# Scores 0 and 1 of an attention tile moved ahead of the transposes of the samples on TensorE

## What is computed

```python
# layer 0: group norm, then a deformable 3x3 convolution: for each pixel and each of 9 taps
offset = conv(x, offset_w) + offset_b         # where to sample
x_off  = g_lt*gather(..) + g_rb*gather(..) + g_lb*gather(..) + g_rt*gather(..)
x = x + conv2d(x_off, conv_w, K, 0)
# layer 1: tokens t (8, 3136, 128)
q, k, v = ln(t) @ Wq.T, ln(t) @ Wk.T, ln(t) @ Wv.T
scores  = where(causal, q @ k.T * C ** -0.5, -inf)
t = t + softmax(scores) @ v
t = t + ffn(ln(t))        # 64 experts, each pools its top 8 tokens of an image
```

## Time and profile before

| what | value |
|---|---|
| median of 3 runs | 4461.97 us (4454.56 to 4466.91) |
| the profiled execution | 4458.19 us |
| its span, first to last instruction | 4456.4 us |
| mean granted TensorE clock | 0.855 of full speed |
| PE busy | 3340.2 us |
| DVE busy | 2008.4 us |
| ACT busy | 1720.8 us |
| POOL busy | 1738.9 us |

### The profile page before, as it was taken

How to read it: one execution, slowest core, us unless ns; L and a number is a source line. 1 busy time by engine, 2 the same in 40 slices (tenths; PEclk the granted TensorE clock), 3 DMA queues, 4 the chain that set the end, 5 groups by cost and what they waited for, 6 DMA issues and landing times. The chain is left out here.

```text
span 4456.4 us, 53569 instructions
## 1 busy us (share of the span) xinstructions
PE 3340.2 (75%) x19490; PEld 2471.3 (55%) x19490; DVE 2008.4 (45%) x7326; ACT 1720.8 (39%) x3764; POOL 1738.9 (39%) x1815
## 2 busy tenths in 40 slices
PE   3267778778777878778787778778777788689469
PEld 1246656556556656556555656556555666567233
DVE  1235544554445544554445444454455445455211
ACT  1234434444443444434344444444444444344100
POOL 1655433544345433544344433544344434520000
PEclk9578889889888889899888989889988898889665
DMA  5423232322323231322323231322322212310565
GB/s 124 147 82 91 69 111 60 96 70 67 111 73 95 72 113 59 100 73 61 114 77 91 72 114 59 96 72 66 109 77 78 71 58 74 88 39 6 209 209 192
DMA packets 261586, 406.03 MB, mean 91 GB/s; under 512 B 43033, under 2 KB 174265, under 8 KB 258251
## 3 DMA queue, kind: packets, MB, share of 16 engines
q0 software_dynamic: 86400, 236.04, 17.9%
q1 hardware_dynamic: 68859, 101.82, 7.3%
q10 hardware_dynamic: 106064, 64.75, 5.3%
HBM read 368.52 MB, written 85.35 MB: 102 GB/s over the span
## 5 line engine op out<-in xcount | busy, mean ns | idle before, releaser
L439 POOL DMA_INDIRECT g<-pair_table,idx x1800 | 1726.7, 959 | 2219.0 <-PE bank_r L956 1597.8
L1000 PE MATMUL bank_o<-vals,prob_t 128*128 128x128 f32 x5200 | 832.9, 312 | 494.9 <-DVE prob_t L718 331.6
L1000 PEld LDWEIGHTS bank_o<-vals,prob_t 128*128 128x128 f32 x5200 | 738.9, 220 | 577.6 <-DVE prob_t L718 374.2
L978 PE MATMUL bank_s<-keys,qt 128*128 128x512 f32 (+3 forms) x1456 | 706.8, 593 | 45.6 <-DVE cmax L711 37.4
L711 DVE CUSTOM_DVE_ANT_0 prob<-bank_s,mask 128x512 f32<-128x512 f32 (+3 forms) x728 | 453.7, 631 | 589.3 <-PE bank_s L978 507.9
L489 ACT ACTIVATE prob_t<-bank_r 128x512 f32<-128x512 f32 (+3 forms) x488 | 267.0, 547 | 1129.6 <-PE bank_r L987 713.0
L964 PE MATMUL bank_conv<-convw_t,smp_t 128*128 128x128 f32 x3600 | 531.3, 298 | 174.9 <-ACT smp_t L482 129.5
L964 PEld LDWEIGHTS bank_conv<-convw_t,smp_t 128*128 128x128 f32 x3600 | 488.6, 211 | 250.8 <-ACT smp_t L482 163.2
L476 ACT ACTIVATE g<-g,wa 128x128 f32<-128x128 f32 x1800 | 564.0, 390 | 32.3 <-DMA g<-pair_table,idx 32.3
L701 DVE SCALAR_TENSOR_TENSOR g<-g,wb 128x128 f32<-128x128 f32 x1800 | 503.0, 345 | 78.3 <-ACT g L476 76.6
L802 DVE TENSOR_TENSOR t<-bank_conv,t 128x128 f32<-128x128 f32 x200 | 58.3, 291 | 996.4 <-remote 701.0
(11 more groups left out here) (152 smaller groups left out, 2609.1 us busy)
## 6 DMA issues: line engine op xcount, KB each, us to landing
pair_table<-in_dram ACTq DMA_DIRECT2D x32, 1568.0 KB
g<-pair_table,idx POOLq DMA_INDIRECT x1800
w1s<-in_dram SPq DMA_DIRECT2D x16, 1024.0 KB, 6.4
w2s<-in_dram SPq DMA_DIRECT2D x16, 1024.0 KB, 9.4
t2s<-t_dram SPq DMA_DIRECT2D x8, 1600.0 KB, 13.2
xpad<-in_dram ACTq DMA_DIRECT2D x8, 1568.0 KB
out_dram<-res SPq DMA_DIRECT2D x8, 1568.0 KB, 6.2
t<-in_dram SPq DMA_DIRECT2D x48, 256.0 KB
```

What stands on the lines that cost most here:

```text
L439: pool.indirect_dma_start(g[t % RING][:, n, :], None, pair_table[b % 2], bass.IndirectOffsetOnAxis(ap=idx[:, b % 2, i * TAPS + n:i * TAPS ...
L978: pe.matmul(bank_s[q % 2][:, 0:w], qt[k % 2][:, at:at + P], key_chunk(tb, k0, w), start=True, stop=True).then_inc(scored, 1)
L1000: last = pe.matmul(attn_ps, prob_t[q % 2][:, n * P:(n + 1) * P], vals[:, slot(tb, at), :], start=(at == 0), stop=(at == ti))
```

## The change

In each step PE now does scores 0 and 1 of the scoring tile first, then the three pieces of `turn_samples`, then score 2 where the tile has three chunks or more. All else, on PE and on the other engines, keeps its order. No wait is added or taken out; the same waits stand at other places of PE's queue.

```diff
@@ -1002,11 +1002,13 @@
                     if c == chunks_in(v) - 1:
                         last.then_inc(attended, 1)
 
+                for c in range(min(chunks_in(ts), 2)):
+                    scores(c)
                 if step < ALL:
                     for p in range(PIECES):
                         turn_samples(p)
-                for c in range(min(chunks_in(ts), 3)):
-                    scores(c)
+                if chunks_in(ts) >= 3:
+                    scores(2)
                 for use in misc_at(step, "E"):
                     fill_misc(use)
                 if step < ALL:
```

## The result

The changed kernel takes 4580.51 us, median of 4 runs (4568.47 to 4598.54); the kernel before took 4458.88 in the same comparison. The ratio is 1.0275 (95% interval 1.0252 to 1.0298): slower by 122 us where +46 was forecast. The direction was right, the size was outside the range.

The account below looks back on a forecast made before the run. PE, 75% busy, was taken to idle in a closed window behind each gather burst. Terms of +63.2, +21.7 and -38.8 gave +46 us: 4504, or 4508 us as median; range 4408 to 4560 for 8 times in 10, own range 4477 to 4545.

Parts of the forecast that it names:

- L802's "remote": DVE's wait at the conv add while the semaphore moved without a just-ended instruction; to fall well below 701.0 us.
- Rival B: The burst's phase does not matter; only PE's 37.4 us of score-bank waits go: 4425 us, chance 0.07.
- 6 to 13: Short-tile steps, without 10: tails grow by the next step's scores, less some takings; +7.9 us an image.
- 1, 2: Steps where PE waits for ACT's query copy or pair-table DMA issue; little or nothing absorbed, +3.1 us together.
- 5, 14: Come out even: in 14 PE is busy beyond the window, in 5 ACT's normalise sets the products' start.
- 15 to 18: Long three-chunk tiles: -0.9 us an image, bank waits gone, and -1.1 more for idle time in 15 and 18.
- 19 to 22: Long four-chunk tiles: 8.5 us of scores in the tail against 6.8 moving ahead, +1.7 us an image.
- 23, 24, 0, 3, 4: Five-chunk long tiles: 10.6 us of scores against 13.6 moving ahead of the block, -3.0 us an image.
- the clock's term: In one long step an image PE's idle time gets short enough for 2.4 GHz to stay: -1.8 us.
- the block: Late-signalled work PE waits for until the burst ends; in step 23 to move from second to third chunk.
- the tail: PE work that waited for the closed window's end; paid in full, two 512-column scores adding 2.12 us a step.
- The window: From about 4.5 to 12.5 us after a gather burst's start, PE's signals reach DVE and ACT late.

Follow-up runs that it names:

- late sets: Sets of runs in which PE's signals arrive late inside a burst of gathers; the kernel before takes 4454 to 4560 us there.
- the prompt pair with gathers in groups: Nine gathers issued in three groups of three, in prompt sets: order of before 3487.63 us (0.9987 of the kernel before), new order 3458.26 us (0.9896).
- prompt sets: Sets of runs in which PE's signals do not arrive late; the kernel before takes 3479 to 3502 us there, the changed kernel 0.9931 of it.
- the copies by hand: Kernel before and changed kernel, each with its first trace's late signals put in as waits: prompt set 4571.63 and 4444.59 us, late set 4688.57 and 4746.27.
- the kernel with the four products: Changed kernel with late signals plus four 384-column products ahead of the third attend, late set: 4800.19 us, 1.0615 of the kernel before.
- one score ahead: Only score 0 ahead of the turns, scores 1 and 2 behind: 3447.86 us, 0.9880 of the kernel before, in a prompt set.
- two in the long steps alone: New order in all steps but 7 to 14 of an image, against the kernel before, prompt sets: 3447.91 us (0.9882) and 3447.02 us (0.9878).

## Why the prediction was right and wrong

**The bottleneck and the mechanism: right in the main.** What the prediction said to look for is there: L802's "remote" far below 701.0 us, L718 within 6 us of the turns' end in step 23 (5.4), the next idle time ahead of the third attend, more idle time in all. Steps 8 and 2 grew by 0.8 and 2.3 us (said: 1 and 2). Rival B is false in the late sets. Where no signal is late its condition holds, and its number comes near: 4425 of 4462 us, 0.992, and the change measured 0.993. That is luck, for its mechanism is not what happens there: PE's waits for a score bank, which were all to go, are 63.3 and 64.7 us in the prompt pair with gathers in groups. The Trainium skill ("Advanced Engine Details and Errata", DMA Bandwidth Details) gives the overhead of a semaphore increment as about one cycle. The prompt sets don't speak against it (the median signal is recorded 13 ns after the instruction's end), the late sets do. The prediction says that the trace agrees outside the burst, but its signal of 2053.30 lies 4.3 us inside the burst, ahead of the stretch in which signals were late.

**The sum: 5.9 us an image was forecast, 21.0 came.** By its terms:

| steps | forecast | measured | of it PE's idle time |
|---|---|---|---|
| 6 to 13 | +7.9 | +10.7 | +6.9 |
| 1, 2 | +3.1 | +2.3 | +1.9 |
| 5, 14 | 0 | +4.4 | +3.5 |
| 15 to 18 | -2.0 | -1.1 | -1.5 |
| 19 to 22 | +1.7 | +5.3 | +4.2 |
| 23, 24, 0, 3, 4 | -3.0 | -0.5 | +0.8 |
| clock | -1.8 | within the others | |
| sum | +5.9 | +21.0 | +15.8 |

As no work was added, all terms but the clock's are idle time of PE: 7.7 us were forecast and 15.8 came. The clock's term is PE's busy time: -1.8 was forecast and +5.2 came. So **two steps of the prediction failed**: the clock's term, 7 of the missing 15 us, and the idle time, 8 of them. Of these 8, 3.5 are steps 5 and 14, which I had put at nothing, and 6.3 the nine steps 19 to 24, 0, 3 and 4; the other classes have 1.7 less than forecast.

These are differences of one trace to one other, and two traces of one kernel differ as well: the kernel before in its other late set (4560.3 us) takes 514.8 us an image, 15.8 more than in the first. What recurs can be seen from the three pairs with late signals, that is the first traces, the copies by hand in the prompt set and those in the late set. Steps 6 to 13 grow in each (+10.7, +9.5, +14.8), steps 5 and 14 too (+4.4, +1.2, +4.0). The long steps go either way (19 to 22: +5.3, -2.0, +0.7; 15 to 18: -1.1, -11.5, +2.6), so their share rests on the first pair alone.

*The clock's term.* I priced the two moved scores at 2.12 us, which is full clock, priced the attend that moves ahead as a gain at full length, and counted 1.8 us an image as saved "where PE's idle time becomes short enough". It did not become short. In step 22 the block ends 13.0 us after the turns' end before and 13.1 in the changed kernel, behind the burst's end both times; what moves ahead of it only lengthens what PE waits in one piece. Step 22, before and changed: two windows each, one ahead of the idle time, one after it to the turns' end (length, five busy times, granted clock, DMA share, GB/s):

```profile
2041.00:2042.60 1.60, 1.54 (x14) 1.30 (x13) 0.00 (x0) 0.00 (x0) 1.21 (x2) 1.00 0.38 128
2045.00:2048.80 3.80, 3.60 (x27) 3.18 (x28) 3.37 (x15) 3.80 (x8) 0.00 (x0) 1.00 0.00 0
```

```profile
2106.60:2110.00 3.40, 2.76 (x24) 2.41 (x22) 0.43 (x2) 1.47 (x4) 2.64 (x3) 1.00 0.35 102
2113.90:2120.10 6.20, 6.13 (x23) 4.30 (x24) 4.39 (x17) 3.83 (x8) 0.00 (x0) 0.64 0.27 85
```

Before, PE had idled 2.41 us and its tail ran at 1.00. In the changed kernel it has idled 3.88 us and the tail runs at 0.64 (a mean of stretches at 2.4 and at 1.2 GHz): one attend takes 2.08 us and the two scores 3.16, where 1.06 and 2.12 were priced. Over the eleven steps 15 to 24 and 0 of that image, from 13.2 us after the turns' end on, the clock was 0.81 in 67.6 us before and 0.68 in 73.1 us after. That is (1 - 0.81) / 0.5 x 67.6 = 25.7 us at half clock before and 46.3 after, of which half is lost: 10.3 us in that image, 8.1 on the mean of the second to the seventh. A part of it comes back elsewhere: in the whole run the turns (L953) took 32 us less and the products (L964) 13. In step 22 the clock is back at 1.00 from 2118.40 on and the turns, now behind the scores, start at 2118.83. So PE's busy time grew by 5.2 us an image. That PE's idle time ahead of the tail goes with the lower clock behind it, the kernel with the four products in that idle time shows: there the clock of the tails rose from 0.73 to 0.89.

*The idle time of the long steps.* I gave each of them credit for what moves ahead of the block (1.1 to 2.7 us), on the reading of step 23 alone and as if the block ended at the same time in both kernels. On the mean of six images the second chunk, the block of before, was copied 12.2, 13.0 and 11.3 us after the turns' end in steps 19 to 21; the third, the block of the changed kernel, is copied at 12.6, 13.5 and 13.1. In step 22 the block moves from the third chunk (12.8) to the fourth (13.1). What moved ahead became idle time. The credit of 5 us an image for PE's waits for a score bank came in part: they fell from 37.4 to 14.8 us in all, but those for the query rose from 2.7 to 15.1, where I had counted one only behind step 9.

*The window was drawn too simply, at little cost.* I let everything through that was signalled before 4.5 us, and a signal or two in the 8 us behind. Step 21 of the changed kernel (turns' end 2080.2, first gather 2080.5) shows how they really pass:

```profile
2084.37 0.48 PE L968 MATMUL bank_conv<-shift,smp_t 9*128 9x128 f32 x2
...
2084.89 0.29 DVE L802 TENSOR_TENSOR t<-bank_conv,t 128x128 f32<-128x128 f32 x1 [3.05 <-PE bank_conv L968]
...
2086.13 0.69 DVE L718 COPY prob_t<-bank_r 128x512 f32<-128x512 f32 x1 [0.40 <-PE bank_r L987]
...
2086.17 1.02 PE L978 MATMUL bank_s<-keys,qt 128*128 128x512 f32 x2
2087.03 1.02 PE L904 MATMUL bank_misc<-keys,wqk 128*128 128x512 f32 x2
...
2087.89 0.60 PE L987 MATMUL bank_r<-ident,prob 128*128 128x128 f32 x4
...
2089.02 0.69 DVE L711 CUSTOM_DVE_ANT_0 prob<-bank_s,mask 128x512 f32<-128x512 f32 x1 [2.19 <-remote]
...
2090.43 0.60 ACT L515 ACTIVATE qt<-bank_misc 128x512 f32<-128x512 f32 x1 [6.03 <-remote]
...
2093.27 0.60 ACT L489 ACTIVATE prob_t<-bank_r 128x512 f32<-128x512 f32 x1 [1.37 <-remote]
...
2093.91 2.89 PE L1000 MATMUL bank_o<-vals,prob_t 128*128 128x128 f32 x14 [4.20 <-ACT prob_t L489]
```

The conv (2084.85) passes at once, the second chunk's signal (2085.4) 0.7 us late, the score's (2087.2) is seen at 2089.02, the query's (2088.05) at 2090.43, the third chunk's (2088.5) only at 2093.27: one by one and in PE's order, here 1.2 to 2.9 us apart. In step 22 the third chunk passes and the fourth is the one held up, to 13.1 us after the turns' end (the copy at 2113.32, see the attend at 2113.97). Whichever is last, the tail begins at the burst's end, so this changes what idles ahead of it and hardly the length of the step. By length steps 5 and 14 missed most, +4.4, and then steps 19 to 22, +3.6.

*Steps 5 and 14* were costed at zero. In step 5 the first attend runs 13.9 us after the turns' end in either kernel, and the idle time ahead of it grew from 1.4 to 3.3 us (mean of six images). That fits a block at the burst's end; whether ACT's normalise, which the prediction named, has a part in it was not separated. *The short steps* came out at +10.7 for +7.9. Steps 6 and 9 have 1.7 us each more than forecast (+2.3 and +3.8), step 13 has 1.1 more and step 11 has 2.6 less. In step 9 the query's product, its copy and the two scores follow one another in the tail (the product took 2.07 us, and the scores 2.50 where 1.47 was priced).

*Two numbers of the prediction.* Scores of 256 and 384 columns were put on a line between two rows, 0.63 and 0.84 us; their own rows give 0.68 and 0.93, which adds 0.2 us an image. And a third off every cost and gain is 41 us either way, 4463 to 4545, not 4477 to 4545.

**What stays open.** The cause of the 2.7% is shown in part: it needs the late signals, and the growth of the short steps comes with them in all three pairs, but the kernels by hand did not bring back the whole. How much of the difference of the long steps is the change and how much the scatter from trace to trace stays open, for the changed kernel without signals by hand has one late trace only. What puts a set of runs into one kind or the other is not known, and nothing in a kernel was seen to do it. That it is the burst that holds the signals up rests on when they are late, not on a run that took the burst away. How the 2.7% divides into parts in a late set is read from the steps' lengths; the parts alone ran only in prompt sets.

**A better version.** In prompt sets one score ahead, or two in the long steps alone, give 0.988, which is below both kernels; whether they are so in a late set was not seen.

## What to carry to other kernels

Where a stall ends at a fixed time, work that fits into it is nearly free and work behind it is paid in full. If the stall's idle time grows, that can be at the lower clock too (in step 22 the tail ran at 1.00 after 2.4 us of idling and at 0.64 after 3.9 us): price moved PE work at the clock of the place to which it goes. The four products fitted into it only in part, and the kernel with them was 54 us slower. Before trusting one trace, run the unchanged kernel again in another set: here the sign of the change hung on which of two conditions the machine was in, and the waits for "remote" were the sign by which to tell them.

## What the hardware showed that was not expected

- The same kernel, 3494.65 us in one set and 4518.18 us in another on one chip; within a set its times lie within 1.3%.
- In late sets 793 to 822 of 2880 PE signals arrived over 0.5 us late, over nine in ten of them inside a burst of nine gathers and the rest up to 3.1 us behind one; in prompt sets 0 to 3.
- In a late set records of updates are missing (2805 and 2776 for 2880 signals; 2881 and more in prompt sets), so single arrivals there are uncertain.
- The level of the late sets comes about from late signals alone: 3493 us became 4572 with them put in by hand, 2.5% above the kernel from whose trace they were taken.
